# Moving the xn transposes to a PSUM bank of their own, beside thirds of FFN2 blocks, and the second FFN1 burst one pair later

## What is computed

```python
xn  = layernorm(x)                                   # (8, 1024, 256)
q = k = v = heads(xn)                                # 16 heads of 16
att = softmax(causal(q @ k.T / 4)) @ v
even, odd = xn[:, 1:17:2], xn[:, 2:17:2]             # 8 tokens each
m1 = outer(even[:, :4], odd[:, :4]).reshape(8, 1024, 256)
m2 = outer(even[:, 4:], odd[:, 4:]).reshape(8, 256, 1024)
h   = gelu(xn @ W1.T + scale * xn @ m1.T + b1)
out = x + att + h @ W2.T + scale * h @ m2.T + b2
```

## Time and profile before

| | |
|---|---|
| median of 3 runs | 940.79 us (940.0 to 941.72) |
| the profiled execution | 942.08 us |
| its span, first to last instruction | 940.3 us |
| PE busy, share of the span | 855.6 us, 91% |
| ACT busy | 682.3 us, 73% |
| DVE busy | 621.6 us, 66% |
| POOL busy | 185.3 us, 20% |
| TensorE clock granted, mean | 0.992 of full |

### The profile page before, as it was taken

One profiled execution on the slowest core, in us unless ns is written; L12 is line 12 of the kernel. 1 busy time (PEld: TensorE's weight loads), 2 busy tenths in 40 slices (PEclk: granted clock), 3 DMA queues, 4 the chain that ended last, 5 costly groups with the idle time before them and its releaser, 6 DMA issues.

```text
span 940.3 us, 17554 instructions
## 1 busy us (share of the span) xinstructions
PE 855.6 (91%) x7040; PEld 485.9 (52%) x7040; DVE 621.6 (66%) x1260; ACT 682.3 (73%) x737; POOL 185.3 (20%) x264
## 2 busy tenths in 40 slices
PE   1689999999999999999999999999999999999994
PEld 1255645656465554646446564555646555465642
DVE  7876695767677596675957668576767759562511
ACT  0547688777878778776887778777787877878782
POOL 1202122120312213121221212212121211212120
PEclk9989999999999999999999999999999999999998
DMA  4845436462373723555353633646246383313113
GB/s 134 298 137 169 144 101 192 130 184 74 102 213 113 241 64 114 145 167 187 102 164 84 203 123 103 191 139 175 73 114 201 114 241 91 107 35 93 38 12 101
DMA packets 212145, 127.18 MB, mean 135 GB/s; under 512 B 139168, under 2 KB 180320, under 8 KB 211040
## 3 DMA queue, kind: packets, MB, share of 16 engines
q1 hardware_dynamic: 212064, 126.06, 45.6%
HBM read 84.02 MB, written 42.01 MB: 134 GB/s over the span
## 4 chain that ended last, share of the span: by engine, by line
PE 72%; ACT 16%; DVE 4%; DMA 2%; issue 2%; POOL 2%; SPq 1%; DVEq 0%; ACTq 0%
PE o_ps L458 27%; PE work L486 15%; PE work L473 14%; PE scores L438 14%; ACT probs L394 13%; ACT L404 2%; POOL probs L386 2%; PE work L498 2%; ACT gelu L404 1%; DMA even<-even_dram 1%; DVE acc L670 1%; DVE xt_w L632 1%; DVE w_lo L599 1%; DMA q_dram<-xt_pair 0%; DMA xn<-x 0%
## 5 line engine op out<-in xcount | busy, mean ns | idle before, releaser
L394 ACT ACTIVATE probs<-scores 128x1024 f32<-128x1024 f32 x576 | 553.5, 1025 | 160.1 <-PE scores L438 159.9
L386 POOL TENSOR_SCALAR_AFFINE_SELECT probs<-probs 128x512 f32<-128x512 f32 x256 | 182.8, 732 | 735.6 <-ACT probs L394 735.6
L458 PE MATMUL o_ps<-probs,v_ones 128*32 128x512 f32 (+3 forms) x3072 | 281.0, 493 | 1.8 <-POOL probs L386 1.7
L438 PE MATMUL scores<-q_stack,k_stack 64*128 64x512 f16 (+3 forms) x1536 | 187.6, 331 | 28.2 <-ACT probs L394 19.3
L486 PE MATMUL work<-w_hi,g_hi 128*128 128x256 f32 x512 | 156.0, 305 | 0.0
L458 PEld LDWEIGHTS o_ps<-probs,v_ones 128*32 128x32 f32 x3072 | 84.1, 109 | 134.4 <-issue 106.6
L486 PE MATMUL work<-w_lo,g_hi 128*128 128x256 f32 x512 | 146.0, 285 | 0.0
L486 PE MATMUL work<-w_hi,g_lo 128*128 128x256 f32 x512 | 145.8, 285 | 0.0
L404 ACT ACTIVATE gelu<-work,b_sb 128x512 f32<-128x512 f32 x128 | 86.5, 688 | 79.2 <-PE work L473 73.4
L438 PEld LDWEIGHTS scores<-q_stack,k_stack 64*128 64x128 f16 x1536 | 51.9, 94 | 164.3 <-ACT probs L394 121.1
L473 PE MATMUL work<-xt_hi,w_hi 128*128 128x512 f32 x256 | 104.9, 410 | 17.4 <-ACT gelu L404 17.4
(11 more groups left out here) (41 smaller groups left out, 543.9 us busy)
## 6 DMA issues: line engine op xcount, KB each, us to landing
q_stack<-q_dram SPq DMA_DIRECT2D x32, 512.0 KB, 4.9
k_stack<-k_dram SPq DMA_DIRECT2D x64, 256.0 KB, 5.2
q_dram<-xt_pair SPq DMA_DIRECT2D x30, 512.0 KB, 4.6
xn<-x SPq DMA_DIRECT2D x16, 512.0 KB, 5.3
w<-w1t SPq DMA_DIRECT2D x8, 1024.0 KB, 7.8
even<-even_dram SPq DMA_DIRECT2D x8, 1024.0 KB, 5.1
xt_w<-w2t SPq DMA_DIRECT2D x8, 1024.0 KB, 5.8
acc<-x SPq DMA_DIRECT2D x8, 1024.0 KB, 7.0
```

Of the source, the lines that this page charges most:

```text
L386: pool.affine_select(out=blk, in_=blk, compare_op=ALU.is_ge, fill=0.0, base=0, pattern=[[0, GH], [1, P]], channel_multiplier=-1).then_inc( ...
L394: act.activation(probs[:, slot % RING, 2 * half:2 * half + 2, :].rearrange("p h q -> p (h q)"), scores[:, half, :], ACT.Exp, scale=EXP_SCA ...
L438: last = pe.matmul(scores[:, half, h * BANK + at:h * BANK + at + n], k_stack[rows, g % 2, half, kb * P:(kb + 1) * P], q_stack[rows, g % 2, ...
L458: last = pe.matmul(o_ps[VW * j:VW * (j + 1), half, q0 % BANK:q0 % BANK + n], v_ones[:, kb, GH * g + j, :], probs[:, slot % RING, j, at:at ...
```

## The change

The bank of a piece no longer follows from turns: FFN2 blocks take bank 0, transposes take bank 1, and FFN1's hidden blocks alternate (block m takes bank m mod 2). Only the transposes ahead of the first batch alternate as before. The second FFN1 burst, `("ffn1", 1)`, goes from pair 9 to pair 10, and the FFN2 parts are laid out anew: thirds of a block (8 matmuls) now stand in pairs 5, 6 and 7, where three of the four transpose pieces are, and halves (12) in pairs 12 and 13. The fourth transpose piece goes from pair 8 to pair 10, ahead of FFN1. DVE's constants move along, most of them by one pair.

```diff
-    10: [("ffn2", 1, 0, 0, 12, 0)],
+    11: [("ffn2", 1, 0, 0, 12, 0)],
 }
 BEHIND = {
...
-    5: [("ffn2", 0, 2, 0, 12, 0), ("xn", 0)],
-    6: [("ffn2", 0, 2, 12, 24, 0), ("xn", 1)],
-    7: [("ffn2", 0, 3, 0, 12, 0), ("xn", 2)],
-    8: [("ffn2", 0, 3, 12, 24, 0), ("xn", 3)],
-    9: [("ffn1", 1)],
-    10: [("ffn2", 1, 0, 12, 24, 0)],
-    11: [("ffn2", 1, 1, 0, 8, 0)],
-    12: [("ffn2", 1, 1, 8, 16, 0)],
-    13: [("ffn2", 1, 1, 16, 24, 0)],
+    5: [("ffn2", 0, 2, 0, 8, 0), ("xn", 0)],
+    6: [("ffn2", 0, 2, 8, 16, 0), ("xn", 1)],
+    7: [("ffn2", 0, 2, 16, 24, 0), ("xn", 2)],
+    8: [("ffn2", 0, 3, 0, 12, 0)],
+    9: [("ffn2", 0, 3, 12, 24, 0)],
+    10: [("xn", 3), ("ffn1", 1)],
+    11: [("ffn2", 1, 0, 12, 24, 0)],
+    12: [("ffn2", 1, 1, 0, 12, 0)],
+    13: [("ffn2", 1, 1, 12, 24, 0)],
...
-LN_STATS, LN_RSTD, LN_APPLY, ADD_B2 = 2, 3, (3, 4), (7, 12)
-SCALE_ODD, ADD_M1, SPLIT_XT, SPLIT_M1, ADD_M2, COPY_V, SPLIT_M2 = 8, 9, 10, 11, 14, 16, 0
+LN_STATS, LN_RSTD, LN_APPLY, ADD_B2 = 2, 3, (3, 4), (7, 9)
+SCALE_ODD, ADD_M1, SPLIT_XT, SPLIT_M1, ADD_M2, COPY_V, SPLIT_M2 = 10, 10, 11, 12, 15, 16, 0
...
-            bank[piece] = turn if kept is None else 1 - kept
-            turn = 1 - bank[piece]
-            bank[piece] = bank[piece], had[bank[piece]]
-            had[bank[piece][0]] += 1
-        if what == "ffn2":
-            kept = bank[piece][0] if key[4] < FFN2_PASSES else None
-        if kept is None or what != "ffn2":
+            first_use = what == "xn" and key[0] == 0
+            at = key[2] % 2 if what == "ffn1" else key[1] % 2 if first_use else int(what == "xn")
+            bank[piece] = at, had[at]
+            had[at] += 1
+        if what != "ffn2" or key[4] == FFN2_PASSES:
```

More of the change, by code:

```diff
@@ L122, in _uses @@
     bank, had, end = {}, [0, 0], {}
-    turn, kept = 0, None
     for what, *key in pieces:
```

## The result

The changed kernel takes 927.1 us (median of 4 runs, 926.86 to 928.69) against 940.39 us for the kernel before, measured beside it (939.99 to 941.72). The ratio is 0.986, with a 95% interval of 0.9843 to 0.9877. The forecast was 924.9 us, with a range from 919.0 to 931.0.

A forecast was written before the change was run, and what follows sets the result against it. PE, busy 91%, bounds pairs with 12 FFN2 matmuls, the scores-exp chain those with 8, both 4.61 us. Gains 11.5 + 0.4 + 8.8 less 4.8 make 15.9 us, forecasting 924.9, range 919.0 to 931.0.

The forecast's parts named there:

- step 5: Pair 14, DVE's queue: splits of xt and w1 take 8.72 us; FFN2 bank free with 1.0 us slack, no cost.
- step 6: Whole kernel: 11.5 + 0.4 + 8.8 - 4.8 = 15.9 us less, giving a median of 924.9.
- 8 and 12 FFN2 matmuls cost a pair the same, and transposes fit beside 8: Pairs 6 and 7: 4.49 us of PE work under a 4.61 exp chain; gain 1.64 a batch, 11.5 us.
- Piece 0 gains nothing outside batch 0: Pair 5: transposes wait for DVE's last xn, staying at 5.1 in batches 1 to 6; batch 0 gains 0.4 us.
- Piece 3 is free ahead of FFN1: Moved from pair 8 to pair 10: pair 8 gains 8.8 us; transposes fit FFN1's 1.04 us idle, cost 0.
- the tie: Pair 10: DVE's pair split ends at 4.4 us, the first gelu also at 4.4; cost 0, at most 3.1.
- the tie on DVE: Pair 10: DVE's piece copy ready at 2.3 us, PE wants the bank at 2.36; cost 0, at most 3.1.
- rival C: Transposes only partly hidden, costing 0.44 us in one to three places: 928.0 to 934.2; chance 0.21.
- The b2 add costs 0.69 us a batch by a late mask: ADD_B2's second half in pair 9: DVE's add delays POOL's second mask of slot 21; costs 4.8 us over seven batches.
- rival D: Pair 14, FFN2's single bank not free: block 2 waits for a late acc; 945.9 if 4 us late; chance 0.03.

The follow-up runs named there:

- banks-only run: The kernel before with only the new banks (FFN2 bank 0, transposes bank 1), all pieces where they were: 929.04 us, ratio 0.9884.

## Why the prediction was right, and where it was off

The sign, the size and the main mechanism came as forecast: 924.9 us predicted, 927.1 measured. One term was mis-sized by 3.2 us (step 5), and some of that was made up by chance (step 6). By the prediction's steps:

1. *8 and 12 FFN2 matmuls cost a pair the same, and transposes fit beside 8.* Right: pairs 6 and 7 at 4.61 and 4.60. The banks-only run splits the gain: the wait for `acc` was 0.86 us in each of two pairs, and transposes on top of twelve FFN2 matmuls cost a pair 0.39. The room was smaller than I had it: I counted 4.49 us of PE work under an exp chain of 4.61, but in pair 6 of the changed kernel PE's own pieces add up to the whole 4.61 (1.86, 0.54, 1.15, 0.44, 0.62), with no idle time. What held is that eight matmuls and the transposes take PE no longer than twelve matmuls.
2. *Piece 0 gains nothing outside batch 0.* Right: 5.10 in batches 1 to 6, 4.61 in batch 0. PE's idle time ahead of the transposes is (14.8 - 12.6) / 6 = 0.4 us, where I had 0.5. Moving the transposes behind the layernorm gained the 0.49.
3. *Piece 3 is free ahead of FFN1.* Right: the gap until the first gelu shrank, and pair 10 without the late mask is 15.22. (In the tie, 1.6 + 2.74 is 4.3 and not 4.4, and the gelu's end is at 4.3 too, so it stays a tie.) PE's timeline in the changed kernel shows the tie on DVE too, at a few hundredths:

```profile
321.65 0.40 PE L470 MATMUL work<-xt_hi,w_lo 128*128 128x512 f32 x1
321.91 0.50 PE L470 MATMUL work<-xt_hi,w_hi 128*128 128x512 f32 x1
...
323.89 0.50 PE L470 MATMUL work<-xt_hi,w_hi 128*128 128x512 f32 x1 [0.32 <-ACT gelu L401]
```

   The cadence is 0.23; hidden block 1 started 0.26 behind the last matmul of block 0, and the 0.32 us of idle time left ahead of block 2 covered what was lost. Its weight load did wait for the copy, 0.3 us at most, which is the sign that I had named for rival C, without C's price.
4. *The b2 add costs 0.69 us a batch by a late mask.* Right in mechanism, 0.66 measured (15.88 less 15.22).
5. *"Slack 1.0 us, no cost", for DVE's queue behind the two splits.* Wrong, on both sides of the comparison. I took the splits' 8.72 us from where they stood before and did not move them against POOL's masks: at the new place they meet more of them and take 9.72. And I compared their end only with the FFN2 bank, wanted 2.4 us into pair 14, and not with the earlier user in the same queue: the evacuation of `o_ps` is wanted when the pair's second slot opens the new group, 0.9 us into the pair at best. With 8.72 us of splits the evacuation would have ended about 0.2 us into pair 14, in time; the 1.0 us that the splits took longer made it late, and only a comparison with this earlier user could have shown that 1.0 us is not there to spare. The argument against rival D, that 8.72 us includes the contention with masks, fails in the same way: it holds for the old place. This cost 0.45 us in seven batches, 3.2 us, and is all but some hundredths of the difference in the steady batches. It is rival D's place with a smaller price and another waiting instruction.
6. *The sum.* 15.9 us less 3.2 gives 12.7, where the medians differ by 13.3; the profiled spans differ by 15.0, of which 1.8 are the first two pairs of batch 0, where the first trace of before was slow. The 0.6 us between 12.7 and 13.3 is not assigned to a cause; outside these two pairs the two traces of the kernel before differ by 0.9. So the forecast is off by 2.2 us and not by 3.2 because 0.6 us more were gained than the steps explain, and because the kernel before took 940.39 instead of 940.79.

## What to carry to other kernels

When a block of work on a side engine moves, list everything queued behind it with the moment at which each is wanted, and take the earliest, not the one that the change is about. Take its duration at the new place, beside its new neighbours. And where the bounding engine has a latency chain with room in it, fill the room first: there, a third of a block plus transposes cost what half a block cost.

## What the runs showed of the hardware

An add of 1,024 float32 elements per partition on DVE, both inputs in SBUF, and a POOL mask exclude each other. Two masks take 1.22 us alone and 2.21 with the add beside them. In the changed kernel's pair 10 the second of them starts at 317.22, while the add runs (316.99 to 318.34), and lasts until 0.5 us behind its end, where an undisturbed mask lasts 0.63:

```profile
317.22 1.62 POOL L383 TENSOR_SCALAR_AFFINE_SELECT probs<-probs 128x512 f32<-128x512 f32 x1
```

In all twelve traces every mask that starts during such an add, 203 of them, ends 0.49 to 0.50 us behind the add's end. Of the two, the one that started first went first. The add went ahead of the second mask wherever it started 0.03 to 0.31 us before that mask did (pairs 3 and 10, and pair 14 in the run with the b2 add there), even where it came 0.46 us behind the start of the first mask, which I had not expected. In pair 12 of the kernel before it was the mask that started first, by 0.1 us, and the add took 1.65 us instead of 1.22.

Shorter DVE instructions take turns with the masks. Beside two masks two of the four subtractions of 512 elements take 1.12 us each instead of 0.69, and the masks 1.12 and 1.08. The casts of 512 elements have a single SBUF input, and were slowed as well: 0.85 us instead of 0.42 for one beside a mask. BN_STATS, with one input, beside the same masks left them at 1.22.

The Trainium skill (SBUF — State Buffer, Who interferes with whom) says that a DVE instruction with two SBUF inputs contends with GpSimd reads and one with a single SBUF input, outside the 2-port modes, does not. The adds, the subtractions and BN_STATS agree. It counts casts among the instructions that can enter the 2-port modes, and the slowed casts fit that, but no run here shows which mode they were in.
